# Rounding of packed counts in two instructions, and 14-bit masks on waited table values, in a four-layer graph network kernel

## What is computed

```python
h = relu(layernorm(x)); x = x + relu((h + segment_sum(h[src], dst)) @ W1 + b1) @ W2 + b2
h = relu(layernorm(x)); x = x + attention(h, edge attributes, src, dst)     # 8 heads, segment softmax
h = relu(layernorm(x)); x = x + h @ w_self.T + b_self + (segment_sum(h[src], dst) / deg) @ w_neigh.T + b_neigh
h = relu(layernorm(x)); x = x + segment_sum(edge_weight * h[src], dst) @ W + b
```

## Time and profile before

| | |
|---|---|
| median of three runs | 5065.54 us (5042.48 to 5067.97) |
| span of the profiled execution, first to last instruction | 5145.3 us |
| mean granted TensorE clock | 0.909 |
| busy: TensorE, VectorE, ScalarE, GpSimd | 75%, 74%, 30%, 53% |

### The profile page before, as it was taken

The page is one execution under the profiler, slowest core; times in us unless marked ns, Lnnn a source line. Parts: engine busy times, 40 slices in busy tenths (PEclk is TensorE's granted clock), DMA queues, the critical chain, the costliest instruction groups (busy, mean ns, idle before and its releaser), DMA issues. The chain is left out here.

```text
span 5145.3 us, 93266 instructions
## 1 busy us (share of the span) xinstructions
PE 3841.6 (75%) x26234; PEld 2720.9 (53%) x26235; DVE 3822.7 (74%) x6359; ACT 1550.3 (30%) x3023; POOL 2737.6 (53%) x2300
## 2 busy tenths in 40 slices
PE   4685555550199968888888888888886348889999
PEld 2443222220189835555555555555554248888888
DVE  3516999991299989999999999999996699970000
ACT  2372234560101130122333444445552430020000
POOL 3430199996732227777777777777776232210000
PEclk8799999995599989999999999999997569999999
DMA  9674423346155444454555666666665535568887
GB/s 168 175 234 111 97 100 126 159 175 198 66 193 209 163 140 106 120 146 142 157 165 169 184 184 188 193 196 197 205 204 159 186 113 200 200 213 300 298 297 254
DMA packets 594376, 912.02 MB, mean 177 GB/s; under 512 B 107452, under 2 KB 519442, under 8 KB 575022
## 3 DMA queue, kind: packets, MB, share of 16 engines
q1 hardware_dynamic: 413024, 521.23, 31.2%
q10 hardware_dynamic: 117359, 250.68, 13.4%
q0 software_dynamic: 63872, 138.75, 11.3%
HBM read 608.33 MB, written 311.94 MB: 179 GB/s over the span
## 5 line engine op out<-in xcount | busy, mean ns | idle before, releaser
L1964 POOL DMA_INDIRECT at_qg<-q_d,at_slot x1616 | 1601.2, 991 | 495.8 <-issue 492.2
L986 PE MATMUL bw_ps<-bw_mov,bw_sta 128*128 128x392 bf16 x7056 | 1590.0, 349 | 19.2 <-issue 7.2
L986 PEld LDWEIGHTS bw_ps<-bw_mov,bw_sta 128*128 128x128 bf16 x7056 | 640.4, 102 | 365.0 <-issue 95.6
L2007 PE MATMUL at_psk<-at_kp,at_hot 128*128 x4848 | 611.7, 234 | 286.8 <-DVE at_qg L2085 244.4
L1051 POOL DMA_INDIRECT tv_rows<-ed_d,tv_place x101 | 628.2, 6219 | 339.1 <-DMA edv_d<-tv_rows 211.0
L2007 PEld LDWEIGHTS at_psk<-at_kp,at_hot 128*128 128x128 bf16 x4848 | 439.1, 101 | 624.1 <-issue 418.1
L889 PE MATMUL ba_ps<-ba_mov,ba_sta 128*128 128x392 bf16 x1968 | 380.4, 338 | 352.6 <-DVE ba_sta L830 309.1
L874 DVE TENSOR_SCALAR ba_mov<-iota,key,scale 128x392 bf16<-128x392 f16 x1968 | 592.4, 365 | 2.8 <-PEq L853 2.8
L970 DVE TENSOR_TENSOR bw_sta<-bw_raw,kw 128x1024 bf16<-128x1024 bf16 x882 | 561.2, 689 | 0.0
L830 DVE TENSOR_TENSOR bw_mov<-bw_ps,lo 128x3136 bf16<-128x3136 f16 x294 | 523.4, 1780 | 7.6 <-PE bw_ps L986 5.4
L1566 PE MATMUL at_p3t<-tile,room 128*128 128x256 f32 (+1 forms) x2450 | 524.2, 376 | 4.6 <-ACT room L1150 4.6
(11 more groups left out here) (537 smaller groups left out, 4668.3 us busy)
## 6 DMA issues: line engine op xcount, KB each, us to landing
tile<-adw_d SPq DMA_DIRECT2D x23, 6272.0 KB, 18.7
adw_d<-xall ACTq DMA_DIRECT2D x65, 1568.0 KB
adj_d<-ba_stage ACTq DMA_DIRECT2D x50, 1568.0 KB, 5.1
l0raw<-adj_d SPq DMA_DIRECT2D x50, 1568.0 KB, 6.6
tile<-adj_d SPq DMA_DIRECT2D x50, 1568.0 KB, 6.5
adw_d<-bw_stage ACTq DMA_DIRECT2D x33, 1568.0 KB
at_rel<-rel_d SPq DMA_DIRECT2D x101, 512.0 KB
et_attr<-in_edge_attr SPq DMA_DIRECT2D x48, 1024.0 KB
```

Of the source, the lines that this page charges most:

```text
L986: ins = pe.matmul(self.ps[:, bass.DynSlice(place, WCOL)], self.sta[:, k, u // 2, :, u % 2], self.mov[:, u // 2, :, u % 2], start=False, st ...
L1964: pool.indirect_dma_start(out=qg[:, ring, b, :], out_offset=None, in_=q_d[:, :], in_offset=bass.IndirectOffsetOnAxis(ap=slot[:, ring, b:b ...
L2007: ins = pe.matmul(ps_k[:, at:at + KW], hot[:, par, sum(ROUNDS[:r]) + u, :], kp[:].rearrange("p j k n -> p (j k n)")[:, bass.DynSlice(place ...
```

## The change

```diff
+TABLE = (1 << 14) - 1
+assert max(NVIS, NVISV, NW + BANKS, NWV + BANKS) <= TABLE
...
@@ CountBuild.visit and WeightBuild.visit (TensorE)
-        pe.wait_ge(self.s_clear, reg)
+        pe.wait_ge(self.s_clear, reg & TABLE)
...
@@ CountBuild.evict (ScalarE)
-                act.wait_ge(self.s_vis, ends[k] + self.ring)
+                act.wait_ge(self.s_vis, (ends[k] & TABLE) + self.ring)
...
@@ WeightBuild.evict (ScalarE)
-                act.wait_ge(self.s_vis, ends[k % half] + self.ring)
+                act.wait_ge(self.s_vis, (ends[k % half] & TABLE) + self.ring)
...
@@ CountLayer.unpack (VectorE)
-        q.odd.inc(ve.tensor_scalar(cast[:, :, HALF:P], raw, ROUND, -ROUND, ALU.add, ALU.add))
+        ve.tensor_scalar(cast[:, 0:NB - 1, HALF:P], raw[:, 0:NB - 1, :], ROUND, -ROUND, ALU.add, ALU.add)
+        q.odd.inc(ve.tensor_scalar(cast[:, NB - 1, HALF:P], raw[:, NB - 1, :], ROUND, -ROUND, ALU.add, ALU.add))
```

## The result

The changed kernel takes 5040.09 us, the median of 14 runs (5033.54 to 5045.64). The kernel before, on the same chip, takes 5067.72 us (14 runs, 5042.48 to 5178.98). The ratio is 0.9943, with a 95% interval of 0.9927 to 0.996. So it is faster, by 28 us (0.55%) where 68 were forecast, just over the 0.5% that can be told from no change, and 42 us slower than the 4998 us predicted.

A forecast was written before the change was run, and what follows sets the result against it. VectorE's unpack was taken to set the count layers' block time, with TensorE the bound after the change. Gains of 25.5 us (first layer) and 42.7 (third), heads and masks 0, make 68: 5065.5 - 68 = 4998 us, range 4975 to 5055.

The forecast's parts named there:

- The rounding: Count layers' unpack on VectorE: 48 rows at the fast rate 1.76 us, last row 0.19, for 3.41; gain 1.54 a block.
- The pace: Time per block in the count layers: 7.65 to 7.07 us in the first, 8.07 to 7.10 in the third.
- The port: Count layers: GpSimd's small instructions and fast VectorE ones exclude each other; up to 0.5 us a block lost on VectorE.
- The rival with a hold of 1.3 us: Count layers: GpSimd holds the port for all of L1385, L1362 waits 1.3 us a block; 5043 us, chance 0.15.
- The heads: Starts of the count layers: shorter unpacks and the bias sum's delay of the rounding cancel; 0, bounds -2 and +2 us.
- The masks: Register operations on TensorE's and ScalarE's sequencers at matrix visits and windows: at most 0.04 us each, taken as 0.
- a cover: Count matrix: TensorE idles 1.44 us ahead of each 8-visit burst; that slack lasts until 0.18 us more a visit.
- the upper bound of 94 us: Weighted matrix: most the masks could cost, 2352 operations at 0.04 us each.
- The range: Whole kernel: 4975 to 5055 us, taking in the port rival and leaving out the no-fast-mode and masks rivals.
- the count layers' rivals: Count layers: port held throughout L1385, 5043 us, chance 0.15; fast mode doesn't engage, 5075 us, chance 0.13.
- the likeliest case's own range: Whole kernel if the forecast case holds, chance 0.64: 4980 to 5015 us, for heads, ties and scatter of runs.
- masks bound the weighted matrix: Weighted matrix: TensorE's sequencer has no slack, 94 us come on the path for 68 gained; 5092 us, chance 0.08.

The follow-up runs named there:

- the kernel with two masks: The changed kernel with a second mask (13 bits, same values) on each visit of the count matrix: 5210.06 us.
- the third set: Runs sharing a chip like the first result's: kernel before 5071.91 us, changed kernel 5038.13, plus thinned-out waits and masks in count visits, weighted visits, or both.
- the weighted visit's by twos: The changed kernel with a wait and a mask once in two visits of the weighted matrix: 5037.93 us in the third set, 6564.52 on the slow chip.
- the fourth set: Runs on the third set's chip: kernel before 5045.45 us, changed kernel 5015.40, masks with one 49-row rounding 5093.20, pauses made on purpose 5148.83.
- the count visit by fours: The changed kernel with a wait and a mask once in four count visits: 6504.14 us on the slow chip; 4961.27 to 5011.93 or 5080.53 to 5091.23 later.
- both together: The changed kernel with wait and mask once in four count visits and once in two weighted visits: 4960.18 to 4967.28 or 5080.37 to 5091.15 us.
- the kernel with pauses made on purpose: The count visit by fours, with VectorE waiting for TensorE one third earlier in the ring: 5148.83 us, ratio 1.0217.

## Why the prediction was right and wrong

**The rounding: right.** 1.75 and 0.19 us for the forecast 1.76 and 0.19; TensorE became the bound, and `output`'s wait went.

**The pace: right in kind, 14 us too small.** First layer 44 x (7.65 - 6.99) = 29.0 for 25.5: the 0.06 us that loop turns lost belonged to VectorE's pace and went with it. Third layer 44 x (8.07 - 6.87) = 52.8 for 42.7: the prediction had taken VectorE's estimated 7.0 us with the port as the pace. It wasn't the bound, and the 6.99 of the earlier trace rows was not yet TensorE's floor.

**The port: right, and smaller than allowed for.** The tie falls one way in each layer. In the first, L1385 waits out the rounding (1.64 us); L1365 then starts 0.1 us ahead of L1388, pays nothing, and L1388 ends 1.1 us behind it. In the third, L1385 slips in before the rounding and is not stretched; L1388 waits out the rounding and is still at work when L1365 starts:

```profile
4300.36 2.53 POOL L1388 TENSOR_SCALAR at_cl_rows<-iota,at_cl_at,row_scale 128x256 f32<-128x256 f16 x1 [0.21 <-POOL at_cl_at L1385]
...
4301.90 3.58 DVE L1365 TENSOR_TENSOR cast<-tile,cast 128x3136 fp32r<-128x3136 f32 x1
```

L1388 ends 0.99 us into L1365, and L1365 loses 0.16 of that (3584 ns for 3426), where up to 0.5 us was allowed. The rival with a hold of 1.3 us is out. The Trainium skill's lock "held for the full instruction" (SBUF — State Buffer, "Terms") fits the first layer and the bias sum, below; it does not fit the third layer.

**The heads: right, 0.** The bias sum shut the rounding out as described, in both layers:

```profile
1362.59 14.78 DVE L1362 TENSOR_SCALAR l0cast<-l0raw 128x3072 fp32r<-128x3072 f32 x1
```
```profile
4143.78 13.68 DVE L1362 TENSOR_SCALAR cast<-tile 128x3072 fp32r<-128x3072 f32 x1
```

**The masks: wrong, and this is the step that made the miss.** It said "at most 0.04 us" an operation, since "a visit now issues at least four things in 0.163 us", and took 0. The operation costs 0.09 us. The number of things issued in an interval was no price for one more ahead of a wait. Why it costs 0.09 us where it is recorded at 0.032 no run shows. For the count matrix the prediction gave a cover that "would go at 0.18 us more a visit". It took all 1.44 us between two bursts for cover. In the burst shown of the kernel with two masks TensorE waited for nobody, and the gap in front of it is still 1.10 us, against 0.24 inside it: going over to the next burst takes TensorE some 0.86 us of its own. An estimate from these rows: with one mask a burst needs 8 x 0.25 + 0.86 = 2.9 us, and VectorE's batches start 2.94 us apart in before (L830 at 906.73 and 909.67). So 0.09 us a visit used the cover up, and VectorE waited for a visit 69 times, 56 us in all. In the third set it is the count visit's masks that show: with these by fours the short runs are 26 to 77 us below the changed kernel, with the weighted visit's by twos nothing changes. For the weighted matrix the upper bound of 94 us was the right kind of number: a second operation there costs some 58 us. The first one's own cost, 26 us between the profiles, does not stand out of the spread of that stage (2291 to 2337 us from the first weighted visit, in the profiles at one mask or fewer).

**What ended the front: not looked at.** The prediction said "In the count matrix VectorE bounds", which a busy VectorE suggested. The first count layer of the profiled before started when the gate was done, and the gate had waited for gathers that stood still beside VectorE. So the front had room for longer visits, and the masks' loss there was smaller than the 138 us by which VectorE's stage ended later (1156 to 1294). In the profiles the front even gained 52 us.

**The sum.** Rounding 81 us gained; masks some 50 lost (48 or 54 in the fourth set) where 0 was taken. 81 - 50 is 31, where 28 were measured. That the rounding gave 14 us more than forecast hid a quarter of the miss, which is luck. The profiled execution of before had a long front. That its timed runs, 78 us shorter, had a shorter one is likely from the two kinds of run seen with the count visit by fours, and with before itself in the third and fourth set, but no profile of a short run was taken.

**The range.** It came from the count layers' rivals and reached upward to 5055, so the time lies in it by luck, for none of those rivals came true; the likeliest case's own range, 4980 to 5015, does not hold it. The rival that "masks bound the weighted matrix" named the right instruction in the wrong stage.

## What to carry to other kernels

A VectorE instruction with one input like this one should have an even number of rows, if one side is dense and the other strided: splitting off the odd row saved almost half of 3.41 us. A register operation ahead of the wait in a loop of short matmul visits cost 0.09 us a visit, not its recorded 32 ns; try it twice in place of once to see whether it is on the path. Before calling an engine the bound of a stage, look at what released the first instruction of the next stage, and at the longest single instruction on each other engine.

## What was not expected of the hardware

- An indirect gather issued by GpSimd stood for 279, 245, 210, 554 and 530 us (normally 0.95). All five are in the four profiles (before, the count visit by fours on two chips, and both together) in which VectorE ran its one-hot matrices without waiting for a visit. In every profile in which VectorE waited for TensorE there, none took over 1.7 us; the kernel with pauses made on purpose shows that the pauses do it. What holds the gather inside the chip no run shows.
- A pause is not the only way through. Three of the five ended with the stage, and two, at 898 and 1026 us, in its middle. Between the two long ones of before, gathers ended one a batch, 0.20 us behind the start of L830, the last instruction of VectorE's batch:

```profile
904.30 2.63 POOL L1051 DMA_INDIRECT tv_rows<-ed_d,tv_place  x1 [0.30 <-issue]
...
906.73 0.67 DVE L830 TENSOR_TENSOR ba_sta<-iota,lo 128x1024 bf16<-128x1024 f16 x1
...
907.23 2.64 POOL L1051 DMA_INDIRECT tv_rows<-ed_d,tv_place  x1 [0.30 <-issue]
...
909.67 0.67 DVE L830 TENSOR_TENSOR ba_sta<-iota,lo 128x1024 bf16<-128x1024 f16 x1
```

- The count visit by fours, with no pauses, has two kinds of run, 4961 to 5012 and 5081 to 5091 us; kernels with pauses agree within 12 to 48 us on the same kind of chip. In the two profiles of the long kind a gather stands until the stage ends; of the short kind no profile was taken on that chip, so what its gathers did is open.
- The same kernel takes 5040 us on one chip and 6591 on another, and the change's sign differs between them: ratio 0.9943 and 1.0223.
